# Attention kernel with gated experts on one core: the value products one head further behind, two casts moved to ScalarE, the first half's sums moved on VectorE

## The chip, the cores and the metric

The kernel runs on one core of one Trainium2 chip. The metric is the device time of one launch in microseconds (us); lower is better. The engines are TensorE (PE in the rows, PEld its weight loads), VectorE (DVE), ScalarE (ACT), GpSimd (POOL) and SyncE (SP), which issues the DMAs.

## What is computed

For 16 batch items of 256 tokens by 256 features, four residual stages, each added to x:

```
x = x + x @ weight[subject].T + bias[subject]
x = x + zX*lap_x(x) + zY*lap_y(x) + zR*x*(1 - x)        # reflected edges
x = x + attention(x, side)    # 16 heads of 16; keys: the masked previous 256 and the token itself
x = x + sum_e w_e * relu(x @ wi_e) @ wo_e               # 2 shared experts and 1 chosen, hidden 1024
        # w = softmax(relu(gate_in @ g1) @ g2), gate_in from token 0 of the three experts
attention: softmax over [q k_prev^T * SCALE (masked), q.k_self * SCALE], times [v_prev, v_self], @ Wo + bo
```

## The kernel before

**Stages and turns.** One pass of the loop is a turn. A turn works on three batch items at once: the inputs, the first two stages and q, k, v of item i; the attention of item i-1 (scores `S0` to `S15`, exponentials `E0` to `E15`); and the experts of item i-2 (`H0` to `H11` the hidden products, `P0` to `P11` the projections). The function `lag` says which item a name belongs to. Turns 0 and 1 are written out, turns 2 to 15 run in a hardware loop, turns 16 and 17 empty the pipeline.

**What sets the order.** Each engine has its own list of names (`PE_BODY`, `ACT_BODY`, `DVE_BODY`, `POOL_BODY`, `SP_BODY`) and works it off strictly from left to right; semaphores join the lists. Nothing is reordered.

**A head.** TensorE makes the transposed scores of head h (`E`, line 665, two matmuls) into one of two PSUM banks. ScalarE takes the exponential twice: to `prob` in f32 (line 869) and to `prob_hi` in f16 (line 873). VectorE (line 1054) or GpSimd (line 1269) subtracts the two into `prob_lo`. For the heads in `HI_DVE` ScalarE takes it only once, and VectorE casts `prob` to `prob_hi` (line 1053) ahead of the subtraction. The tuple `LO_DVE` holds the heads whose `prob_lo` VectorE makes; the other nine are GpSimd's. There are three buffers of each (`NPROB`), taken in turn by h % 3. The function `attend` multiplies head h by the values: eight matmuls of 49 columns (lines 607 and 608, "pv" in the rows), which wait for `prob_lo` of h. It is called right behind `E` of head h + `BEHIND`, and `pvend` calls it for the heads that are left over.

**Banks.** The two front banks go round in the order of TensorE's list (`RING`): `E14` uses the bank in which `kp` stood, and waits until VectorE has read that (line 1014, `beside<-front`). `kp` uses the bank of `E11`; `E11` that of `lap`.

**The first half's sums.** `half` on VectorE (lines 1062, 1065, 1067) reads the value products of heads 0 to 7 from PSUM. It waits for `attend` of head 7. `attend` of head 8 writes over the same PSUM and waits for `half` (the semaphore `pv_freed`). `lap` on VectorE (line 1003) adds the Laplacian from PSUM to `react`; `x2_parts` (line 976) then splits the result of the second stage, on which TensorE's `kp` waits.

**GpSimd's list** in this part of the turn is `E8 E9 E10 qa E12 norm qb E14`: four subtractions of `prob_lo`, two of q (lines 1230 and 1233), and the first half's normalisation (lines 1259 and 1263).

The lists around the change, before:

```
PE   ... m1 E7 x1 P7 q E8 H9 E9 lap P8 E10 H10 E11 E12 kp E13 P9 E14 E15 H11 P10 pvend P11 vs ...
ACT  ... x1_parts react q E8 P7 H9 E9 x2_parts E10 qa H10 E11 E12 kp E13 qb kq E14 E15 H11 P11 ...
```

Of the kernel before, what the change touches and what calls it, by code (L numbers as in the profile page):

```python
# [67 lines left out]
ACT_FIRST = "x_parts w_parts s_parts x1_parts react q qa x2_parts qb kp kq vs ks vp x2b".split()  # L68
DVE_BODY = """
H0 S0 S1 H1 S2 S3 S4 S5 H2 S6 S7 S8 S9 H3 S10 S11 H4 H5 S12 S13 E1 S14 H6 S15 E3 H7 E5 gate0 x_parts H8 E7  # L70
x1 x1_parts react half lap H9 x2_parts gate1 E11 H10 kp E13 k3 E15 H11
att gate2 aT relu wo logits x3_parts mix scale vp self
""".split()
POOL_BODY = """
# [20 lines left out]
def family(name):  # L95

    if name in FAMILIES:
        return name, 0
    return (name[0], int(name[1:])) if name[0] in FAMILIES and name[1:].isdigit() else (None, 0)
# [23 lines left out]


NPROB = 3
BEHIND = 2
HI_DVE = (11, 13, 15)
LO_DVE = (1, 3, 5, 7) + HI_DVE
N_LO_DVE = [sum(g in LO_DVE for g in range(h + 1)) for h in range(H)]
N_LO_POOL = [h + 1 - N_LO_DVE[h] for h in range(H)]  # L130

# [2 lines left out]

LINKS = {"early": 3, "attention": 4 + 5 + len(HI_DVE), "rest": 8}


def wait(eng, sem, per_turn, turn, n):

    value = turn * per_turn + n  # L140
    if isinstance(value, int) and value <= 0:
        return
    eng.wait_ge(sem, value)


def build(nc, x, side, seq_len, subject, label, z, w0, b0, wqkvo, vecs, wi, wo, swi, swo,
          g1, g2, consts, iota, out):
    with ExitStack() as ctx:
# [204 lines left out]
        def wait_freed(eng, i, name):  # L353
            kind, n = family(name)
            wait(eng, freed[kind], FAMILIES[kind], i, n + 1)

        def wait_prob_split(eng, i, h):

            if h in LO_DVE:
                wait(eng, prob_split_dve, N_LO_DVE[-1], i, N_LO_DVE[h])  # L360
# [186 lines left out]
        def _(pe):  # L547
# [48 lines left out]
            def attend(i, h):  # L596

                wait_prob_split(pe, i, h)
                if h == 0:
                    wait(pe, v_split, 1, i, 1)  # L600
                if h == HALF:
                    wait(pe, pv_freed, 1, i, 1)
                for t in range(C):
                    acc = pv[:, t, (h % HALF) * VW:(h % HALF + 1) * VW]
                    for k in range(C):
                        at = k * S + t * P
                        nc.tensor.matmul(acc, prob_hi[:, h % NPROB, at:at + P], v_cols[:, k, h, :], start=(k == 0), stop=False)  # L607
                        last = nc.tensor.matmul(acc, prob_lo[:, h % NPROB, at:at + P], v_cols[:, k, h, :],
                                                start=False, stop=(k == C - 1))
                last.then_inc(pv_done, 1)  # L610

            def front(name, i):
                if name == "pvend":
                    for h in range(H - BEHIND, H):
                        attend(i, h)
# [51 lines left out]
                last.then_inc(filled[family(name)[0]], 1)  # L667
                if name[0] == "E" and int(name[1:]) >= BEHIND:
                    attend(i, int(name[1:]) - BEHIND)

# [117 lines left out]
        def _(act):  # L788
            def front(name, i):
# [73 lines left out]
                elif name[0] == "E":  # L863
# [5 lines left out]
                    last = nc.scalar.activation(prob[:, h % NPROB, :], psum[:, :], ACT.Exp, scale=SCALE)  # L869
                    if h not in HI_DVE:  # L870
                        if h >= NPROB:
# [89 lines left out]
        def _(dve):  # L961
# [9 lines left out]
            def front(name, i):  # L971
# [76 lines left out]
                elif name[0] == "E":  # L1048
                    h = int(name[1:])
                    wait_freed(dve, i, name)  # L1050
                    if h in HI_DVE:
                        wait(dve, pv_done, H, i, h - NPROB + 1)
# [290 lines left out]
```

## Time and profile before

| what | value |
| --- | --- |
| time, median of 3 runs | 1078.11 us (1074.57 to 1078.93) |
| the profiled execution, its own time | 1079.35 us |
| its span, first to last instruction | 1077.5 us |
| PE busy | 993.3 us, 92% |
| DVE busy | 828.2 us, 77% |
| ACT busy | 670.6 us, 62% |
| POOL busy | 623.9 us, 58% |
| one turn in the dense part (540.0 to 602.8 us) | 62.8 us, of which PE is busy 60.24, DVE 51.01, ACT 41.18, POOL 37.74 |
| granted TensorE clock in it | 1.00 of full |

Matmuls overlap in the engine, so the start of one to the start of the next is what it costs, not its duration. A row of the timeline gives a start, a duration, and in square brackets how long the engine had sat idle before it and what ended that.

### The profile page before, as it was taken

Reading aid. Unit: us, or ns where it says so; the run is one execution under the profiler, and the core shown is the slowest. Engines: PE = TensorE matmul, PEld = TensorE weight load, DVE = VectorE, ACT = ScalarE, POOL = GpSimd, SP = SyncE. Lnnn points to the kernel's source line nnn. Section 1 sums busy time; section 2 is a strip of 40 time slices with the busy share of each in tenths; the row PEclk is TensorE's granted clock in tenths of the full one; section 3 lists DMA queues with packets and bytes.
Section 4 is the critical chain, followed back from the end, with each engine's and each line's share of the span. In section 5 each row is a group of like instructions: output and inputs, shape, how many; then the busy total and the mean of one; then the engine's idle time right before and its main releaser. Section 6 shows DMA issues by size and latency. Waiting matters only on the chain.

```text
span 1077.5 us, 27626 instructions
## 1 busy us (share of the span) xinstructions
PE 993.3 (92%) x9488; PEld 926.5 (86%) x9488; DVE 828.2 (77%) x1584; ACT 670.6 (62%) x1403; POOL 623.9 (58%) x548
## 2 busy tenths in 40 slices
PE   5669999999999999999999999999999999999896
PEld 5358989898998989899898989989898998989886
DVE  6566787878878787887878788787878878787633
ACT  4464756667485666748566674856667485666641
POOL 5683646567374656737465673746567374655440
PEclk8568999999999999999999999999999999999988
DMA  6626142531614253162425316242531614252110
GB/s 159 164 71 118 51 60 79 91 85 46 111 59 59 79 90 86 45 110 61 59 79 90 86 44 111 61 59 79 88 88 44 110 62 59 79 89 59 41 49 10
DMA packets 91387, 82.68 MB, mean 77 GB/s; under 512 B 11972, under 2 KB 90852, under 8 KB 91364
## 3 DMA queue, kind: packets, MB, share of 16 engines
q1 hardware_dynamic: 91364, 82.38, 35.7%
q8 instruction: 14, 0.23, 0.1%
q14 instruction: 9, 0.07, 0.0%
HBM read 52.59 MB, written 4.20 MB: 53 GB/s over the span
## 4 chain that ended last, share of the span: by engine, by line
PE 33%; issue 25%; POOL 22%; DVE 14%; ACT 3%; SPq 1%; DMA 1%; POOLq 0%; DVEq 0%; ACTq 0%
POOL exp_lo L1212 12%; PE front L550 3%; PE hid L550 3%; PE front L552 3%; PE front L551 3%; POOL prob_lo L1269 3%; PE hid L552 3%; PE hid L551 3%; PE out L550 3%; PE out L552 3%; PE out L551 3%; DVE gate_terms L1133 2%; DVE prob_lo L1054 2%; DVE prob_hi L1053 2%; PE pv L607 2%
## 5 line engine op out<-in xcount | busy, mean ns | idle before, releaser
L1269 POOL TENSOR_TENSOR prob_lo<-prob,prob_hi 128x512 f16<-128x512 f32 x144 | 174.4, 1211 | 108.6 <-ACT prob_hi L873 108.6
L550 PE MATMUL hid<-x_hi,exp_hi 128*128 128x256 f32 x768 | 230.1, 300 | 1.5 <-DVE x_lo L1114 1.5
L550 PE MATMUL out<-hid_hi,exp_hi 128*128 128x256 f32 x768 | 228.2, 297 | 0.0
L551 PE MATMUL hid<-x_lo,exp_hi 128*128 128x256 f32 x768 | 217.1, 283 | 0.0
L552 PE MATMUL hid<-x_hi,exp_lo 128*128 128x256 f32 x768 | 216.9, 282 | 0.0
L551 PE MATMUL out<-hid_lo,exp_hi 128*128 128x256 f32 x768 | 214.7, 280 | 0.0
L552 PE MATMUL out<-hid_hi,exp_lo 128*128 128x256 f32 x768 | 214.6, 279 | 0.0
L1212 POOL TENSOR_TENSOR exp_lo<-raw,exp_hi 128x512 fp32r<-128x512 f32 x128 | 169.3, 1337 | 70.3 <-ACT exp_hi L890 70.2
L1034 DVE TENSOR_REDUCE s_max<-front 128x2 f32<-128x512 f32 x256 | 167.7, 687 | 46.2 <-PE front L652 44.2
L912 ACT ACTIVATE hid_hi<-hid 128x512 fp32r<-128x512 f32 x192 | 114.8, 598 | 111.6 <-PE hid L552 110.3
L1118 DVE SCALAR_TENSOR_TENSOR hid_lo<-hid,hid_hi 128x512 fp32r<-128x512 f32 x192 | 131.6, 685 | 64.5 <-ACT hid_hi L912 64.2
L869 ACT ACTIVATE prob<-front 128x512 f32<-128x512 f32 x256 | 151.4, 598 | 39.6 <-PE front L665 36.8
L550 PEld LDWEIGHTS hid<-x_hi,exp_hi 128*128 128x128 f32 x768 | 145.6, 190 | 4.0 <-DVE x_lo L1114 1.6
L550 PEld LDWEIGHTS out<-hid_hi,exp_hi 128*128 128x128 f32 x768 | 144.4, 188 | 3.2 <-DVE hid_lo L1118 0.2
L551 PEld LDWEIGHTS hid<-x_lo,exp_hi 128*128 128x128 f32 x768 | 146.1, 190 | 0.0
L552 PEld LDWEIGHTS hid<-x_hi,exp_lo 128*128 128x128 f32 x768 | 145.6, 190 | 0.0
L551 PEld LDWEIGHTS out<-hid_lo,exp_hi 128*128 128x128 f32 x768 | 144.8, 189 | 0.0
L552 PEld LDWEIGHTS out<-hid_hi,exp_lo 128*128 128x128 f32 x768 | 144.3, 188 | 0.0
L1054 DVE TENSOR_TENSOR prob_lo<-prob,prob_hi 128x512 f16<-128x512 f32 x112 | 113.6, 1014 | 31.2 <-ACT prob_hi L873 29.5
L607 PEld LDWEIGHTS pv<-v_cols,prob_hi 128*128 128x128 f16 x1024 | 70.6, 97 | 65.3 <-DVE prob_lo L1054 36.5
L607 PE MATMUL pv<-v_cols,prob_hi 128*128 128x49 bf16 x1024 | 87.2, 187 | 42.2 <-DVE prob_lo L1054 27.7
L873 ACT ACTIVATE prob_hi<-front 128x512 f16<-128x512 f32 x208 | 125.0, 601 | 0.0
(166 smaller groups left out, 2329.0 us busy)
## 6 DMA issues: line engine op xcount, KB each, us to landing
raw<-in_wi SPq DMA_DIRECT2D x64, 256.0 KB, 3.7
raw<-in_wo SPq DMA_DIRECT2D x64, 256.0 KB, 2.8
q_rows<-w_raw SPq DMA_DIRECT2D x80, 128.0 KB, 4.0
k_rows<-x1T SPq DMA_DIRECT2D x48, 128.0 KB, 5.0
k_rows<-x_raw SPq DMA_DIRECT2D x48, 128.0 KB, 6.1
x_raw<-in_x SPq DMA_DIRECT2D x16, 256.0 KB, 2.9
w_raw<-in_w SPq DMA_DIRECT2D x16, 256.0 KB, 2.8
s_raw<-in_side SPq DMA_DIRECT2D x16, 256.0 KB, 3.7
```

The lines of the kernel that those rows point to most:

```text
L550: nc.tensor.matmul(acc, w_hi, a_hi, start=first, stop=False)
L551: nc.tensor.matmul(acc, w_hi, a_lo, start=False, stop=False)
L552: return nc.tensor.matmul(acc, w_lo, a_hi, start=False, stop=last)
L607: nc.tensor.matmul(acc, prob_hi[:, h % NPROB, at:at + P], v_cols[:, k, h, :], start=(k == 0), stop=False)
L869: last = nc.scalar.activation(prob[:, h % NPROB, :], psum[:, :], ACT.Exp, scale=SCALE)
L873: last = nc.scalar.activation(prob_hi[:, h % NPROB, :], psum[:, :], ACT.Exp, scale=SCALE)
L912: nc.scalar.activation(hid_hi[:, s % 2, :], hid_bank[s % 2][:, :], ACT.Relu).then_inc(hid_hi_done, 1)
L1034: nc.vector.tensor_reduce(s_max[:, :, h:h + 1], psum, AX_X, ALU.max).then_inc(freed["S"], 1)
L1054: nc.vector.tensor_tensor(prob_lo[:, h % NPROB, :], prob[:, h % NPROB, :], prob_hi[:, h % NPROB, :], ALU.subtract).then_inc(prob_split_dve, 1)
L1118: nc.vector.scalar_tensor_tensor(hid_lo[:, s % 2, :], hid_bank[s % 2][:, :], 0.0, hid_hi[:, s % 2, :].bitcast(F32), ALU.max, ALU.subtract) ...
L1212: nc.gpsimd.tensor_tensor(lo, source, hi.bitcast(F32), ALU.subtract).then_inc(w_split, 1)
L1269: nc.gpsimd.tensor_tensor(prob_lo[:, h % NPROB, :], prob[:, h % NPROB, :], prob_hi[:, h % NPROB, :], ALU.subtract).then_inc(prob_split_poo ...
```

## The change

`BEHIND` goes from 2 to 3, so that `attend` of head h stands behind `E` of head h+3, and `pvend` holds three heads, not two. Heads 13 and 15 leave `HI_DVE`: ScalarE takes their second exponential into `prob_hi`, and VectorE no longer casts them; `LO_DVE` is unchanged in content. `half` moves on VectorE's list from in front of `lap` to behind `H9`.

```
-x1 x1_parts react half lap H9 x2_parts gate1 E11 H10 kp E13 k3 E15 H11
+x1 x1_parts react lap H9 half x2_parts gate1 E11 H10 kp E13 k3 E15 H11
...
 NPROB = 3
-BEHIND = 2
-HI_DVE = (11, 13, 15)
-LO_DVE = (1, 3, 5, 7) + HI_DVE
+BEHIND = 3
+HI_DVE = (11,)
+LO_DVE = (1, 3, 5, 7, 11, 13, 15)
```

VectorE in the loop, around `lap` (L1003), `H9` (L1118), the first half's sums (L1062 to L1067) and `x2_parts` (L976):

```order
+L1003 SCALAR_TENSOR_TENSOR react<-front,z_sb,react 128x512
+L143 REGISTER_ALU
+L1118 SCALAR_TENSOR_TENSOR hid_lo<-hid,hid_hi 128x512
 L1062 TENSOR_REDUCE att<-pv 128x128 x2
 L1065 TENSOR_TENSOR den<-pv,p_self 128x2x8
 L1067 RECIPROCAL den<-den 128x2x8
-L1003 SCALAR_TENSOR_TENSOR react<-front,z_sb,react 128x512
-L143 REGISTER_ALU
-L1118 SCALAR_TENSOR_TENSOR hid_lo<-hid,hid_hi 128x512
 L976 TENSOR_TENSOR x_lo<-react,x_hi 128x512
```

Two operations that stood behind the sums now stand ahead of them; `x2_parts` keeps its place right behind.

VectorE in the loop, from the reading of `kp` (L1014, `beside`) on, heads 13 and 15:

```order
 L1014 SCALAR_TENSOR_TENSOR beside<-front,ebias,x1T 128x256 x2
-L1053 CAST prob_hi<-prob 128x512
-L143 REGISTER_ALU
 L1054 TENSOR_TENSOR prob_lo<-prob,prob_hi 128x512
 L143 REGISTER_ALU
...
 L1020 TENSOR_TENSOR x_raw<-beside,x_raw 128x256
-L1053 CAST prob_hi<-prob 128x512
-L143 REGISTER_ALU
 L1054 TENSOR_TENSOR prob_lo<-prob,prob_hi 128x512
```

The two casts behind `kp` are gone; the cast of head 11, ahead of it, stays.

ScalarE in the loop, head 13 behind the two parts of `kp`, ahead of `qb` (L822) and `kq` (L838):

```order
 L869 ACTIVATE prob<-front 128x512
+L873 ACTIVATE prob_hi<-front 128x512
 L822 ACTIVATE w_raw<-s_raw 128x512
 L838 ACTIVATE x_raw<-beside 128x256 x2
...
 L869 ACTIVATE prob<-front 128x512
+L873 ACTIVATE prob_hi<-front 128x512
 L143 REGISTER_ALU
 L912 ACTIVATE hid_hi<-hid 128x512
```

One more exponential stands ahead of `qb` (head 13) and one ahead of `H11` (head 15).

## Rows read from the trace of the kernel before

**Rows 1.** The page: busy time by engine, and the costliest-groups row of line 607.

```profile
PE 993.3 (92%) x9488; PEld 926.5 (86%) x9488; DVE 828.2 (77%) x1584; ACT 670.6 (62%) x1403; POOL 623.9 (58%) x548
...
L607 PE MATMUL pv<-v_cols,prob_hi 128*128 128x49 bf16 x1024 | 87.2, 187 | 42.2 <-DVE prob_lo L1054 27.7
```

**Rows 2.** Timeline of PE: start, duration, operation, [idle before it and releaser].

```profile
138.91 0.20 PE L607 MATMUL pv<-v_cols,prob_hi 128*128 128x49 bf16 x1 [1.03 <-DVE prob_lo L1054]
...
560.62 0.38 PE L665 MATMUL front<-q_rows,k_rows 100*128 100x256 bf16 x2
561.14 0.20 PE L607 MATMUL pv<-v_cols,prob_hi 128*128 128x49 bf16 x1
...
573.03 0.19 PE L607 MATMUL pv<-v_cols,prob_hi 128*128 128x49 bf16 x1
...
575.88 0.20 PE L607 MATMUL pv<-v_cols,prob_hi 128*128 128x49 bf16 x1 [0.30 <-POOL prob_lo L1269]
...
579.03 0.20 PE L607 MATMUL pv<-v_cols,prob_hi 128*128 128x49 bf16 x1 [1.01 <-DVE prob_lo L1054]
...
580.75 0.39 PE L665 MATMUL front<-q_rows,k_rows 100*128 100x256 bf16 x2
580.98 0.19 PE L607 MATMUL pv<-v_cols,prob_hi 128*128 128x49 bf16 x1
...
582.32 0.20 PE L607 MATMUL pv<-v_cols,prob_hi 128*128 128x49 bf16 x1 [0.75 <-DVE prob_lo L1054]
...
582.54 0.35 PE L550 MATMUL hid<-x_hi,exp_hi 128*128 128x256 f32 x1
...
585.88 0.36 PE L550 MATMUL out<-hid_hi,exp_hi 128*128 128x256 f32 x1
...
956.26 0.20 PE L607 MATMUL pv<-v_cols,prob_hi 128*128 128x49 bf16 x1 [1.03 <-DVE prob_lo L1054]
```

**Rows 3.** Timeline of DVE in the same turn, from the first half's sums on.

```profile
570.87 0.56 DVE L1062 TENSOR_REDUCE att<-pv 128x128 f32<-128x384 f32 x1 [0.26 <-PE pv L608]
...
572.17 0.66 DVE L1003 SCALAR_TENSOR_TENSOR react<-front,z_sb,react 128x512 f32<-128x512 f32 x1
...
573.53 0.88 DVE L976 TENSOR_TENSOR x_lo<-react,x_hi 128x512 fp32r<-128x512 f32 x1
...
574.84 1.26 DVE L1133 SCALAR_TENSOR_TENSOR gate_terms<-gate,e_out,gate_terms 128x256 f32<-128x256 f32 x1
...
576.13 1.28 DVE L1053 CAST prob_hi<-prob 128x512 f16<-128x512 f32 x1
577.44 1.53 DVE L1054 TENSOR_TENSOR prob_lo<-prob,prob_hi 128x512 f16<-128x512 f32 x1
...
579.50 0.86 DVE L1014 SCALAR_TENSOR_TENSOR beside<-front,ebias,x1T 128x256 f32<-128x256 f32 x2
```

**Rows 4.** Timeline of POOL in turn 1 (first row) and in the same turn as rows 2.

```profile
76.22 0.73 POOL L1259 TENSOR_TENSOR att<-att,v_self 128x256 f32<-128x256 f32 x1
...
574.54 1.27 POOL L1269 TENSOR_TENSOR prob_lo<-prob,prob_hi 128x512 f16<-128x512 f32 x1 [0.69 <-ACT prob_hi L873]
575.78 1.34 POOL L1230 TENSOR_TENSOR s_raw<-q_full,w_raw 128x512 f32<-128x512 f32 x1
577.10 1.32 POOL L1269 TENSOR_TENSOR prob_lo<-prob,prob_hi 128x512 f16<-128x512 f32 x1
578.39 1.17 POOL L1259 TENSOR_TENSOR att<-att,v_self 128x256 f32<-128x256 f32 x1
579.64 0.40 POOL L1263 TENSOR_TENSOR att<-att,den 128x128 f32<-128x128 f32 x1
```

**Rows 5.** Timeline of ACT in the same turn, the second exponential of head 12.

```profile
576.40 0.62 ACT L873 ACTIVATE prob_hi<-front 128x512 f16<-128x512 f32 x1
```

**Rows 6.** Timeline of PE in turn 1, the first with attention.

```profile
50.76 0.22 PE L607 MATMUL pv<-v_cols,prob_hi 128*128 128x49 bf16 x1 [2.38 <-POOL prob_lo L1269]
...
78.54 0.28 PE L665 MATMUL front<-q_rows,k_rows 100*128 100x256 bf16 x1 [1.27 <-DVE beside L1014]
```

## The prediction

> **What bounds the kernel now.** The page first: TensorE is busy 92% of the span and no other engine more than 77% [rows 1]. Idle time on TensorE is therefore what a reordering can win. The costliest single wait of it is ahead of the value products, 42.2 us in all, 27.7 of them for a `prob_lo` of VectorE [rows 1]. The timeline of TensorE over one turn then shows where. Four waits come back in every turn: 0.29 us ahead of the products of head 4 (its `E6` starts at 560.62 and costs 0.23, as from 580.75 to 580.98, yet the products start only at 561.14), 0.30 for head 10, 1.01 for head 11, 0.75 for head 13 [rows 2]. That is 2.35 us of a turn. The wait of head 11 stands in 14 turns, the first at 138.91 and the last at 956.26: 13 periods of 62.87 us [rows 2]. Everything else in those turns has TensorE packed, so a turn costs what its path from wait to wait costs. The four waits together are 14 x 2.35 = 33 us, the most that the change could take away in the dense part.
>
> **What goes.** With `attend` one head further behind, each of the four waits meets a `prob_lo` that was made one head earlier, and all four go. For that to be a gain, the work behind them must be ready earlier too. Up to `E10` it is: the lists there are TensorE-driven, and I shift everything by the 0.29 of head 4. From `E10` on, the path goes over to VectorE, for which I follow one turn in the trace's own times.
>
> **The path from the half's sums to `E14`.** The products behind `E10`, at 573.03 before [rows 2], are now those of head 7, at 572.74. Their eight matmuls need 0.36 us to the end, and the semaphore 0.1: `half` can start at 573.20. Before, it started at 570.87 [rows 3]. `lap` and `H9` now run ahead of it, but VectorE has only those two (0.66 and 0.68 us) to fill the time, so it stands idle for about 1.5 us where it had idled 0.26. `half` costs 572.17 - 570.87 = 1.30 us [rows 3], and so `x2_parts` may begin at 574.50, against 573.53 before. (`pv_freed` comes inside those 1.30 us, and the products of head 8 want it at 574.70. No stall there, with 0.2 us to spare. ScalarE's second exponential waits for the products of head h-3, which now stand behind its own `E`: they are done 0.36 us behind `E`, and the first exponential takes longer than that.)
>
> What comes then is the costly part, because GpSimd works without a gap from 574.54 to 580.0 [rows 4], and VectorE operations on SBUF operands do not run beside it. The cast at 576.13 took 1.28 us: it ended at 577.41, 0.29 us after GpSimd's operation ended (575.78 + 1.34 = 577.12). The subtraction at 577.44 ended at 578.97, 0.55 us after 577.10 + 1.32 = 578.42. The gate term at 574.84 ended 0.29 after 574.54 + 1.27 [rows 3, 4]. So each such operation costs the rest of GpSimd's operation, then 0.29 or 0.55 us. Operations that read PSUM (`half`, `H10`, the reading of `kp`) keep their length.
>
> GpSimd's own times: its subtraction for head 10 moves from 574.54 to 574.17, since `x2_parts` on ScalarE no longer holds up that head's exponentials. Unhindered it would last 1.17 us, to 575.34. Then:
>
> - `x2_parts`, ready at 574.50, waits for 575.34 and ends at 575.89. TensorE's `kp` starts at 575.99, against 576.10 (575.88 and 0.22 of products) before [rows 2]: so far 0.11 us won out of the first 0.59 of waits.
> - The first gate term waits for GpSimd's `qa`, 575.31 + 1.34 [rows 4] = 576.65, perhaps 0.25 more as it had to let a 512-wide operation by. It ends at 577.0 to 577.2. Before, this one ran freely.
> - The second gate term meets the subtraction of head 12. That depends on ScalarE's exponential (576.40, now 0.28 earlier: ended 576.74 [rows 5]) and on `qa`, and runs to about 578.05. The term ends at 578.35.
> - The cast of head 11 meets the addition of `norm`. That took 1.17 us where it let a subtraction by, and 0.73 in turn 1 [rows 4]; I take 0.8, to 578.9. The cast ends at 579.2.
> - The subtraction of head 11 meets one of the two 0.40 us multiplications of `norm` [rows 4], to about 579.35, and ends at 579.9.
> - From there to the end of reading `kp` it is, as before, 579.50 + 0.86 - 578.97 = 1.39 us [rows 3]: 581.29. The casts that are taken away (heads 13 and 15) stand behind this point, so they give nothing here.
>
> `E14` on TensorE needs that bank, and starts at 581.33, against 580.75. TensorE, which has won 2.35 us of waits, gets to it at about 579.4 and stands there for 1.9 us. This is the new wait.
>
> **From `E14` to `P11`.** Before: 585.88 - 580.75 = 5.13 us, 0.75 of it the wait for head 13 [rows 2]. Now `E14` and `E15` at 0.23 each, two products at 0.21, then `H11` and `P10` (585.88 - 582.54 = 3.34, with two products in it) and one more product, 0.21: 4.43 us. `P11` starts at 581.33 + 4.43 = 585.76, against 585.88. On the way VectorE must have `hid_lo` of `H11` ready: its two casts less pay for ScalarE's additional exponential of head 15 (0.6 us), and I find it ready at 585.5, so it is covered by 0.3 us. ScalarE has 62.8 - 41.2 us free in a turn; the two exponentials more hide there. Net: 0.12 us won in a turn, 14 x 0.12 = 1.7 us. The break-even is `E14` at 581.45, and nearly every microsecond of the forecast hangs on whether the chain above ends before or after it.
>
> **The ends.** Turn 1 is not dense: TensorE waits 2.38 us for the first subtraction with `E3` stuck behind it, and 1.27 us at `E14` [rows 6]. There `E3` comes up to 1.4 us earlier (the exponential of head 3 needs only the buffer of head 0), and `lap` ahead of `half` gives `E11` 0.7 us. Bounds 0 and 4, I take 2.5 us. The last attention turn has few waits left: 0.3 us.
>
> **The sum.** 1.7 + 2.5 + 0.3 = 4.5 us. On the profiled execution's own 1079.35 us (span 1077.5 and 1.85 around it) that gives 1074.9; it lies 1.2 above the median of the runs, 1078.11, from which it is **1073.6 us**.
>
> **The rule on the shared port.** The rows above show VectorE waiting for GpSimd's whole operation. The Trainium skill, page "SBUF — State Buffer", section "SBUF: two separate sides", states it for both sides: the pair of ports is an exclusive lock, held for the full instruction, and the loser blocks entirely. The trace agrees for VectorE; for GpSimd it does not quite, since the operation next to the cast took 1.32 us and not the 1.16 + 0.3 of a full block [rows 4].
>
> **Rivals.**
>
> 1. *VectorE's chain ends later (slower).* Each VectorE operation that squeezes in holds GpSimd up by its whole 0.3 to 0.55 us, not by 0.1 to 0.2, and the five operations of the stretch add about 1 us: `E14` at 582.3. From `E14` at 582.0 on, the loss in 14 turns outweighs 0.5% and the gain of the ends. At 582.3 it is 14 x 0.85 - 2.8 = 9 us lost: 1087. For it: GpSimd has no gap in the stretch, and one more of its operations (`qb`, 1.3 us) waits behind. Against: the 1.32 above. By that rule of the Trainium skill ("SBUF — State Buffer") in its full form, this would be the case. Chance 0.2.
> 2. *One VectorE operation escapes.* A gate term or the cast that starts before GpSimd's next operation does runs in 0.4 us; the cast spent 0.99 us of its 1.28 waiting [rows 3, 4]. Then the path is 0.9 shorter: 14 x 0.9 more, 1061 to 1064. For it: the second gate term and the subtraction of head 12 start within 0.2 us of each other. Chance 0.23. Without any such waits `E14` would be bound by TensorE, 14 x 2.1 + 3: 1046; I leave that out.
> 3. *The waits only change place.* The four go, `E14` takes up all of them, turn 1 is bound by GpSimd as before: 1078. Chance 0.15.
>
> The forecast itself has 0.42, with a range of 1069 to 1078.
>
> **Numbers.** A measurement of this kernel can tell about 0.5% from no change, which is 5.4 us: 1072.7 and 1083.5. Faster by more: all of rival 2 and a little less than half of the forecast's own, 0.42. Slower by more: rival 1, 0.2. Within: the rest, 0.38. The range reaches from rival 2 to short of the worst of rival 1: 1063 to 1086.
>
> **What would show it.** In the changed trace: the four waits of the value products gone from TensorE's list, and in their place one wait per turn of `front` (line 665) for VectorE's `beside` (line 1014), 1.9 us by this sum. VectorE idle about 0.8 us ahead of the sums of line 1062. The gate terms and the cast between them at 1.2 us each, not 0.4. The period of a turn at 62.7 us: above 63.0 is rival 1, under 62.2 is rival 2. The forecast falls if `kp` or the products of head 8 wait instead (the 0.2 us to spare on `pv_freed` is the thinnest cover), or if `P11` comes to wait for `hid_lo`.

## The result, and the profile after

The changed kernel takes 1086.73 us in the median of 5 runs (1083.17 to 1087.27), against 1075.93 for the kernel before in the same comparison (5 runs). The ratio is 1.0086, with a 95% interval of 1.0061 to 1.0110: slower by 0.9%. The forecast was 1073.6 and its range ended at 1086. The profiled execution has a span of 1085.4 us, against 1077.5.

From the page of the changed kernel, the busy time and the group that now has the large wait (the same columns as in [rows 1]):

```profile
PE 997.6 (92%) x9488; PEld 943.5 (87%) x9488; DVE 800.5 (74%) x1552; ACT 683.4 (63%) x1435; POOL 628.6 (58%) x548
...
L665 PE MATMUL front<-q_rows,k_rows 100*128 100x256 bf16 x512 | 102.3, 282 | 39.7 <-DVE beside L1014 29.6
```

VectorE is busy 28 us less, ScalarE 13 more: the casts moved. The 42.2 us ahead of the value products [rows 1] are no longer the largest wait. The list of waits of TensorE says what took their place (in total, times, longest):

```profile
PE front L665 <- DVE beside L1014: 29.6, 15, 2.1
PE front L550 <- DVE x_lo L976: 9.7, 15, 2.1
...
PE front L658 <- DVE s_max L1034: 5.7, 15, 2.0
```

That is one wait per turn at `E14` (line 665) and one at `kp` (line 550). The wait at `kp` is new too: 0.55 us a turn. The forecast's numbers hold one of about 0.5 (0.59 us won ahead of it, and `kp` only 0.11 earlier), though its list of signs names a wait at `kp` as one that would make it fall. In the timeline of TensorE, one dense turn of the changed kernel reads as follows; it is the turn to be laid beside [rows 2], with `kp`, `E14`, `H11`, `P10` and `P11`:

```profile
579.49 0.35 PE L550 MATMUL front<-x_hi,lin_hi 128*128 128x256 f32 x1 [0.55 <-DVE x_lo L976]
...
585.09 0.39 PE L665 MATMUL front<-q_rows,k_rows 100*128 100x256 bf16 x2 [2.01 <-DVE beside L1014]
...
585.94 0.51 PE L550 MATMUL hid<-x_hi,exp_hi 128*128 128x256 f32 x1
...
588.60 0.41 PE L550 MATMUL out<-hid_hi,exp_hi 128*128 128x256 f32 x1
...
591.01 0.37 PE L550 MATMUL out<-hid_hi,exp_hi 128*128 128x256 f32 x1
```

So far this is the forecast: the four waits are gone, and one of 2.01 us (1.9 was written) stands at `E14`. Then something the forecast does not have: `H11` to `P10`, twelve matmuls of 256 columns, takes 588.60 - 585.94 = 2.66 us. Before, it took 584.03 - 582.54 [rows 2] = 1.49, with `P10` starting in this row of the kernel before:

```profile
584.03 0.28 PE L550 MATMUL out<-hid_hi,exp_hi 128*128 128x256 f32 x1
```

The windows show why. They cover the pause, the 3.4 us that begin 0.9 us behind it, and 3.4 us later on; the columns are busy us of PE, PEld, DVE, ACT and POOL with the instructions, then the granted clock, the DMA share and GB/s:

```profile
584.00:585.00 1.00, 0.00 (x0) 0.00 (x0) 1.00 (x4) 0.00 (x0) 1.00 (x1) 1.00 0.00 0
586.00:589.40 3.40, 3.40 (x20) 3.40 (x17) 1.09 (x2) 2.29 (x5) 1.17 (x1) 0.50 0.54 112
590.00:593.40 3.40, 3.40 (x49) 3.36 (x48) 2.18 (x8) 0.66 (x2) 0.00 (x0) 1.00 1.14 127
```

TensorE is idle while VectorE and GpSimd work. Then its granted clock is 0.50 (1.2 GHz) for 3.4 us, in which it is called fully busy, yet a matmul of 256 columns starts every 0.22 us (2.66 / 12) instead of every 0.12 (1.49 / 12). (The 49 matmuls of the last window can't be set against the 20: many of them are value products of 49 columns.) `E14` to `P11` takes 591.01 - 585.09 = 5.92 us, against the 4.43 of the forecast, which all belonged to the full clock. Not every turn has this. `E14` of five successive turns, the last but one being the row at 585.09 above:

```profile
393.90 0.28 PE L665 MATMUL front<-q_rows,k_rows 100*128 100x256 bf16 x1 [2.01 <-DVE beside L1014]
...
458.13 0.28 PE L665 MATMUL front<-q_rows,k_rows 100*128 100x256 bf16 x1 [2.01 <-DVE beside L1014]
...
522.36 0.28 PE L665 MATMUL front<-q_rows,k_rows 100*128 100x256 bf16 x1 [2.00 <-DVE beside L1014]
...
649.30 0.28 PE L665 MATMUL front<-q_rows,k_rows 100*128 100x256 bf16 x1 [2.00 <-DVE beside L1014]
```

The distances are 64.23, 64.23, 62.73 and 64.21 us. A turn without the slow stretch takes 62.7 us, and one with it 1.5 us more; 10 of the 14 turns from 2 to 15 have one. In the kernel before none of these turns has one, and a turn takes 62.87. The slow stretch does not begin at a fixed distance from the pause: in the ten turns it begins 0.4 to 1.6 us behind the pause's end.

The account of the 7.9 us between the two spans, with a turn counted from the first matmul of `x1`: up to the x1 stage of turn 2, 3.4 us are won (120.33 us instead of 123.75). In the next 13 turns, 9 slow stretches cost 9 x 1.52 = 13.7 us and the shorter path wins 13 x 0.16 = 2.1. The rest (turn 15, with the tenth slow stretch, and the emptying of the pipeline) is 0.3 us shorter. -3.4 + 13.7 - 2.1 - 0.3 = 7.9.

VectorE's chain in the same turn, for [rows 3], and GpSimd's subtraction of head 10, `qa` and subtraction of head 12, for [rows 4]:

```profile
576.60 1.02 DVE L1062 TENSOR_REDUCE att<-pv 128x128 f32<-128x384 f32 x2 [0.60 <-PE pv L608]
...
577.90 1.43 DVE L976 TENSOR_TENSOR x_lo<-react,x_hi 128x512 fp32r<-128x512 f32 x1
579.26 2.69 DVE L1133 SCALAR_TENSOR_TENSOR gate_terms<-gate,e_out,gate_terms 128x256 f32<-128x256 f32 x2
581.99 0.85 DVE L1053 CAST prob_hi<-prob 128x512 f16<-128x512 f32 x1
582.87 0.77 DVE L1054 TENSOR_TENSOR prob_lo<-prob,prob_hi 128x512 f16<-128x512 f32 x1
...
584.17 0.86 DVE L1014 SCALAR_TENSOR_TENSOR beside<-front,ebias,x1T 128x256 f32<-128x256 f32 x2
```

```profile
577.63 1.16 POOL L1269 TENSOR_TENSOR prob_lo<-prob,prob_hi 128x512 f16<-128x512 f32 x1 [0.62 <-ACT prob_hi L873]
578.75 1.62 POOL L1230 TENSOR_TENSOR s_raw<-q_full,w_raw 128x512 f32<-128x512 f32 x1
580.33 1.34 POOL L1269 TENSOR_TENSOR prob_lo<-prob,prob_hi 128x512 f16<-128x512 f32 x1
```

`x_lo` takes 1.43 us instead of 0.88: GpSimd's subtraction, already running, ends at 577.63 + 1.16 = 578.79, and `x_lo` 0.54 later. The two gate terms take 2.69 us together, behind `qa` and the subtraction of head 12 in the same way. This is as the forecast had it. From the start of the sums (576.60) to the end of reading `kp` (585.03) it is 8.43 us; the walk of the prediction had 581.29 - 573.20 = 8.09.

### The profile page after: what moved, and what is told of

It reads as the page before. It is cut to its first block, busy times and chain, and to the rows that moved or that the text cites. A ratio compares the mean times of both kernels' runs of the same rounds, so it can differ in the third digit from the quotient of the medians.

```text
span 1085.4 us, 27581 instructions
## 1 busy us (share of the span) xinstructions
PE 997.6 (92%) x9488; PEld 943.5 (87%) x9488; DVE 800.5 (74%) x1552; ACT 683.4 (63%) x1435; POOL 628.6 (58%) x548
## 4 chain that ended last, share of the span: by engine, by line
PE 73%; DVE 18%; issue 3%; POOL 2%; ACT 1%; DMA 1%; SPq 1%; DVEq 0%; ACTq 0%
PE hid L550 8%; PE hid L551 8%; PE hid L552 7%; PE out L550 7%; PE out L552 7%; PE out L551 7%; PE front L665 5%; PE front L652 4%; PE front L550 4%; DVE gate_terms L1133 3%; PE front L552 3%; PE front L551 3%; DVE s_max L1034 3%; PE pv L607 2%; DVE x_lo L976 2%
## 5 line engine op out<-in xcount | busy, mean ns | idle before, releaser
L550 PE MATMUL hid<-x_hi,exp_hi 128*128 128x256 f32 x768 | 234.2, 305 | 1.8 <-DVE x_lo L1114 1.8
L551 PE MATMUL hid<-x_lo,exp_hi 128*128 128x256 f32 x768 | 221.3, 288 | 0.0
L552 PE MATMUL hid<-x_hi,exp_lo 128*128 128x256 f32 x768 | 221.1, 288 | 0.0
L1118 DVE SCALAR_TENSOR_TENSOR hid_lo<-hid,hid_hi 128x512 fp32r<-128x512 f32 x192 | 131.7, 686 | 72.1 <-ACT hid_hi L912 71.1
L550 PEld LDWEIGHTS hid<-x_hi,exp_hi 128*128 128x128 f32 x768 | 149.1, 194 | 4.3 <-DVE x_lo L1114 1.9
L551 PEld LDWEIGHTS hid<-x_lo,exp_hi 128*128 128x128 f32 x768 | 150.3, 196 | 0.0
L552 PEld LDWEIGHTS hid<-x_hi,exp_lo 128*128 128x128 f32 x768 | 149.9, 195 | 0.0
L873 ACT ACTIVATE prob_hi<-front 128x512 f16<-128x512 f32 x240 | 144.9, 604 | 0.0
L665 PE MATMUL front<-q_rows,k_rows 100*128 100x256 bf16 x512 | 102.3, 282 | 39.7 <-DVE beside L1014 29.6
L1054 DVE TENSOR_TENSOR prob_lo<-prob,prob_hi 128x512 f16<-128x512 f32 x112 | 92.1, 823 | 47.0 <-ACT prob_hi L873 45.1
L1236 POOL TENSOR_TENSOR ksT<-ksT,q_full 128x512 f32<-128x512 f32 x16 | 20.4, 1278 | 129.4 <-ACT ksT L808 129.4
```

The costliest lines, as they stand in the source:

```text
L550: nc.tensor.matmul(acc, w_hi, a_hi, start=first, stop=False)
L551: nc.tensor.matmul(acc, w_hi, a_lo, start=False, stop=False)
L552: return nc.tensor.matmul(acc, w_lo, a_hi, start=False, stop=last)
L665: last = nc.tensor.matmul(psum[:, k * S:(k + 1) * S], k_rows[0:ROWS_EXP, h, k * P:(k + 1) * P], q_rows[0:ROWS_EXP, h, :], start=True, stop ...
L873: last = nc.scalar.activation(prob_hi[:, h % NPROB, :], psum[:, :], ACT.Exp, scale=SCALE)
L1054: nc.vector.tensor_tensor(prob_lo[:, h % NPROB, :], prob[:, h % NPROB, :], prob_hi[:, h % NPROB, :], ALU.subtract).then_inc(prob_split_dve, 1)
```

## The experiments

Theories. **Clock**: the loss is the slow stretch of TensorE behind the new pause. **Path**: the loss is VectorE's longer chain itself (rival 1 of the prediction), and the clock is only a companion. Ratios are against the kernel before in the same comparison. "Slow stretches" counts turns 2 to 15 with a stretch of granted clock 0.50, in the one profiled execution of each kernel. Each median is of 3 to 10 executions, but of 2 for e10_fill_behind, e13_fill_far and e14_pause, and the two of e14_pause lie 6.7 us apart.

| kernel | median us | ratio, 95% interval | slow stretches of 14 | dense turn, us |
| --- | --- | --- | --- | --- |
| before | 1075.9 | 1 | 0 | 62.87 |
| changed | 1086.7 | 1.0086 (1.0061 to 1.0110) | 10 | 62.7 or 64.2 |
| e1_fill | 1071.3 | 0.9941 (0.9920 to 0.9961) | 0 | 62.7 |
| e9_fill_4 | 1071.8 | 0.9949 (0.9933 to 0.9965) | 0 | 62.7 |
| e10_fill_behind | 1103.7 | 1.0246 (1.0225 to 1.0267) | 3 | 64.7 or 66.2 |
| e13_fill_far | 1101.6 | 1.0243 (1.0213 to 1.0273) | 11 | 63.7 or 65.2 |
| e14_pause | 1101.8 | 1.0245 (1.0171 to 1.0319) | 5 | 63.8 or 65.3 |
| e5_no_casts | 1087.8 | 1.0095 (1.0079 to 1.0112) | 10 | 62.9 or 64.2 |
| e6_half_back | 1098.5 | 1.0195 (1.0178 to 1.0212) | 10 | 63.8 to 65.7 |
| e7_half_alone | 1083.2 | 1.0050 (1.0033 to 1.0067) | 0 | 63.1 |
| e3_casts | 1063.5 | 0.9879 (0.9863 to 0.9896) | 0 | 61.9 |
| e8_all_casts | 1061.2 | 0.9858 (0.9841 to 0.9874) | 0 | 61.7 |
| e2_h11_ahead | 1069.0 | 0.9922 (0.9905 to 0.9938) | 0 | 62.46 |
| e4_gate1_later | 1068.5 | 0.9917 (0.9900 to 0.9933) | 0 | 62.42 |
| e11_h11_everywhere | 1081.9 | 1.0046 (1.0032 to 1.0060) | 7 | 62.55 or 64.0 |
| e12_casts_gate1 | 1074.1 | 0.9976 (0.9966 to 0.9985) | 0 | 62.6 |

### The pause filled

On TensorE, in turns 2 to 15, ahead of `E14`:

```
+FILL = 16
...
+                if name == "E14" and not isinstance(seq, int):
+                    for _ in range(FILL):
+                        nc.tensor.matmul(hid_bank[1][:, 0:S], lap_mats[:, 0:P], lap_mats[:, :], start=True, stop=True)
```

> The changed kernel with 16 extra matmuls (128x256, f32r, constants, result overwritten by the next hidden product) between P9 and E14 in turns 2 to 15, where TensorE pauses for 2.0 us. They do no work for the result and end before the pause did. Clock theory (the loss is that the granted clock falls to 1.2 GHz behind this pause in two of three turns, which costs 1.5 us each time): the clock stays at 1.00 through turns 2 to 15, every turn takes 62.7 us instead of 64.2, and the time falls by about 10 x 1.5 = 15 us to some 1071. Path theory (the loss is the later end of VectorE's chain): E14 starts where it did, nothing changes, 1086. If the filler ends too late, turns are a few tenths longer in both.

It came out at 1071.3 us, on the expectation of the clock theory. `E14` starts 18.07 us behind the first matmul of `x1`, where it also started in the changed kernel (585.09 - 567.01 = 18.08), but no pause is left ahead of it (line numbers are up to 4 higher in kernels with a filler):

```profile
513.77 0.39 PE L666 MATMUL front<-q_rows,k_rows 100*128 100x256 bf16 x2
```

The granted clock over the dense turns, in windows, e1_fill:

```profile
130.00:960.00 830.00, 816.15 (x8071) 780.45 (x8069) 652.85 (x1273) 553.21 (x1177) 504.04 (x437) 1.00 0.37 75
```

and the changed kernel:

```profile
130.00:960.00 830.00, 792.00 (x7707) 756.83 (x7707) 641.57 (x1251) 545.77 (x1160) 495.35 (x431) 0.98 0.36 75
```

TensorE does 224 more matmuls for nothing, and the kernel is 15 us faster, because the clock is 1.00 and not 0.98. VectorE's chain is as long as before. The path theory falls with this run: with the clock kept up, the change as a whole is a gain of 0.6% (0.4% to 0.8%), and the 4.5 us of the prediction, 0.42%, lie at the near end of that.

### A smaller filler, and two controls

Four extra matmuls instead of 16:

```
-FILL = 16
+FILL = 4
```

> As the filled kernel, with 4 extra matmuls in the pause instead of 16, so that about 1.55 us of the 2.0 us pause are left, in one piece. If the clock falls on the length of the pause in steps, the count of 1.2 GHz stretches in turns 2 to 15 lies between the 10 of the changed kernel and the 0 of the filled one, and the time between 1071 and 1086 at 1.5 us for each stretch; E14 starts where it did in both.

No slow stretch at all, with 1.55 us of the pause left:

```profile
514.38 0.28 PE L666 MATMUL front<-q_rows,k_rows 100*128 100x256 bf16 x1 [1.55 <-DVE beside L1018]
```

So 0.45 us of work in the pause bought 15 us. The expectation of something in between was wrong: 14 pauses of 1.55 us lowered the clock in no turn.

The same 16 behind `E14`, outside the pause:

```
-                if name == "E14" and not isinstance(seq, int):
+                if name == "E15" and not isinstance(seq, int):
```

> The control to the filled kernel: the same 16 extra matmuls per turn, but between the products behind E14 and E15, so the pause of 2.0 us ahead of E14 stays whole. Clock theory (the pause, not the amount of work in a turn): the 1.2 GHz stretches come back in most turns; a turn takes 62.7 + 1.9 = 64.6 us without one and 1.5 to 3 more with one: 1110 to 1118. If more work in a turn alone kept the clock up: 64.6 in every turn, 1098.

```profile
529.00 0.28 PE L666 MATMUL front<-q_rows,k_rows 100*128 100x256 bf16 x1 [2.04 <-DVE beside L1018]
```

The pause is whole, and the slow stretches are back, but only 3, and the time of 1103.7 lies between the two expectations. That left open whether more work in a turn also protects. A second control has 8 extra matmuls ahead of `H4`, 28 us from the pause:

```
+FILL = 8
...
+                if s == 4 and not isinstance(j, int):
+                    for _ in range(FILL):
+                        nc.tensor.matmul(psum[:, 0:S], lap_mats[:, 0:P], lap_mats[:, :], start=True, stop=True)
```

> A second control: the changed kernel with 8 extra matmuls (0.95 us) ahead of H4 in turns 2 to 15, some 28 us away from the pause ahead of E14, which stays 2.0 us. Clock theory (what stands in the pause matters): 1.2 GHz stretches in most turns again, 7 to 11 of 14, turns of 63.7 us without and 65.2 with one, time about 1100. If more work anywhere in a turn protected the clock: none, 63.7 in every turn, 1085.

```profile
528.56 0.37 PE L666 MATMUL front<-q_rows,k_rows 100*128 100x256 bf16 x1 [2.00 <-DVE beside L1018]
```

11 slow stretches and 1101.6 us, as the clock theory expects. More work in a turn does not protect by itself; work in the pause does. Why the same pause of 2.0 us lowered the clock 10 or 11 times in three kernels, but 3 times in the control with the filler right behind it, is not settled. One thing that no run here varied by itself is the length of a turn (62.7 to 64.7 us in these kernels), and with it where the pause falls in time.

### The converse

In the kernel with the two casts alone (below), TensorE waits ahead of `E14` for VectorE's `k3`, in turns 2 to 15:

```
+                if name == "E14" and not isinstance(seq, int):
+                    wait(pe, k_split, 1, seq + 1, 1)
```

> The converse, in the fastest kernel but one (the kernel before with the two casts on ScalarE): TensorE waits ahead of E14 for VectorE's k3, which ends about 1.9 us after TensorE gets there; nothing else is changed, BEHIND is 2. Clock theory: one pause of about 2 us makes 1.2 GHz stretches in many of turns 2 to 15 where there were none; a turn is 61.9 + 1.9 = 63.8 us without one and 1.5 more with one, time 1097 to 1104. If the clock fell in the changed kernel for another reason (its order of products, say), no stretches here: 1090.

```profile
523.70 0.20 PE L607 MATMUL pv<-v_cols,prob_hi 128*128 128x49 bf16 x1 [1.04 <-DVE prob_lo L1056]
...
527.31 0.28 PE L665 MATMUL front<-q_rows,k_rows 100*128 100x256 bf16 x1 [1.74 <-DVE x_raw L1022]
```

The added pause is 1.74 us long, in a kernel with `BEHIND` 2 and the sums where they were, and 5 slow stretches come where there were none. It does not stand alone: the wait of 1.04 us for head 11 ends at 523.70, and the pause begins 1.9 us later, so the run shows what the two do together. A turn is 63.8 us without a slow stretch and 65.3 with one, the same 1.5 us. Most of what this kernel loses against the casts alone (38 us in the medians) is the pause itself, 14 x 1.9 = 27 us by the turns; the five stretches are about 8.

### The parts of the change

The casts alone (`BEHIND` 2, `half` ahead of `lap`):

```
-HI_DVE = (11, 13, 15)
-LO_DVE = (1, 3, 5, 7) + HI_DVE
+HI_DVE = (11,)
+LO_DVE = (1, 3, 5, 7, 11, 13, 15)
```

> The kernel before with one part of the change alone: the high parts of heads 13 and 15 on ScalarE; BEHIND stays 2 and the sums stay ahead of the Laplacian. By the trace of before: VectorE's subtraction of head 13 starts at once behind the reading of kp and ahead of GpSimd's qb, so it ends about 1 us earlier and the wait of 0.75 us ahead of the products of head 13 goes; nothing behind it is later. Clock theory: the waits left are 0.3, 0.3 and 1.0 us, the clock stays at 1.00, and the turn falls to about 62.1: 14 x 0.75, time about 1066. Path theory: the same, since VectorE's path is shorter. If instead this part is the harmful one, slower than before, since ScalarE's qb and kq are 0.5 us later: 1080 or more.

1063.5 us: 1.2% faster than before, and better than expected. In VectorE's timeline of the kernel with the casts alone, the subtraction of head 13 takes 0.68 us right behind the reading of `kp`:

```profile
510.71 0.86 DVE L1014 SCALAR_TENSOR_TENSOR beside<-front,ebias,x1T 128x256 f32<-128x256 f32 x2
511.49 0.68 DVE L1054 TENSOR_TENSOR prob_lo<-prob,prob_hi 128x512 f16<-128x512 f32 x1
```

It begins just ahead of GpSimd's `qb` and does not wait for it; behind the cast it had waited. The wait of 0.75 us at head 13 [rows 2] is gone, and the turn is 0.95 us shorter.

The other two parts without the casts:

```
-HI_DVE = (11,)
-LO_DVE = (1, 3, 5, 7, 11, 13, 15)
+HI_DVE = (11, 13, 15)
+LO_DVE = (1, 3, 5, 7) + HI_DVE
```

> The changed kernel with the casts of heads 13 and 15 back on VectorE: the one further head behind and the moved sums alone. VectorE's chain up to the reading of kp is untouched by those casts, so the pause ahead of E14 stays 2.0 us and the granted clock falls behind it in most turns. Clock theory: as slow as the changed kernel, 1084 to 1089; the 0.95 us per turn that the casts alone gave is hidden under the wait for the bank. Path theory with the casts as an independent gain: 13 us slower than the changed kernel, about 1100.

```profile
PE front L665 <- DVE beside L1014: 29.5, 15, 2.1
```

1087.8 us, as slow as the changed kernel (1086.7), with the same wait. The casts, worth 13 us alone, are worth about 1 us inside the change, which the intervals do not tell from nothing: the pause at `E14` hides what they save. The slow stretch costs 1.3 us here, 64.25 us against 62.95.

One head further behind, with the sums back ahead of the Laplacian:

```
-x1 x1_parts react lap H9 half x2_parts gate1 E11 ...
+x1 x1_parts react half lap H9 x2_parts gate1 E11 ...
```

> The changed kernel with the sums back ahead of the Laplacian, one head further behind kept. VectorE then waits for the products of head 7 (now behind E10) before it can do lap, about 2.6 us idle, and E11, x2_parts on ScalarE, the exponentials of head 10 and kp come later by 0.7 to 1.5 us. Dense turns of 64 us without clock falls; with pauses ahead of E11, kp and E14 that add up to 4 us the clock also falls in most turns: 1100 to 1110. If the moved sums were what cost the time, it would be faster than the changed kernel: 1075 or less.

```profile
PE front L665 <- ACT prob_hi L873: 20.7, 22, 1.3
PE front L550 <- ACT prob L869: 12.2, 14, 0.9
PE front L665 <- DVE react L1003: 10.7, 15, 2.4
```

1098.5 us, 1.5 under the expected range. `E11` waits for `lap` (0.6 us a turn), `E12` and `kp` for ScalarE (1.04 and 0.90), and the clock falls in 10 turns, behind the second of these waits or behind the third. In 4 of the 10 the slow stretch lasts 6.8 us and not 3.4. So the moved sums are needed once the products are three heads behind.

The moved sums alone, in the kernel before:

```
-x1 x1_parts react half lap H9 x2_parts gate1 E11 ...
+x1 x1_parts react lap H9 half x2_parts gate1 E11 ...
```

> The kernel before with the moved sums alone. The products of head 8, behind E10, now wait about 0.9 us for the sums, which start 1.9 us later than before; x2_parts and the gate terms meet GpSimd's operations one place later, so the reading of kp is later by up to 1 us and shows in the wait of head 11. Dense turns of 63.6 to 64 us, no single pause over 1.3 us, so the clock stays at 1.00: 1088 to 1094.

```profile
PE pv L607 <- DVE den L1065: 13.5, 15, 2.5
PE pv L607 <- DVE prob_lo L1054: 11.1, 31, 1.1
```

The wait for the sums is there (0.81 us a turn), but the turn is only 0.25 us longer and not 0.7 to 1.1, since part of the later waits for `prob_lo` falls under it (11.1 us left of them). 1083.2, and no slow stretch. The expectation overstated what follows.

### Towards a faster kernel

All three casts on ScalarE, `BEHIND` 2:

```
-HI_DVE = (11, 13, 15)
-LO_DVE = (1, 3, 5, 7) + HI_DVE
+HI_DVE = ()
+LO_DVE = (1, 3, 5, 7, 11, 13, 15)
```

> The kernel before with the casts of all three heads, 11, 13 and 15, on ScalarE (the last run's faster part, taken one head further). The cast of head 11 costs VectorE 1.3 us there, 1.0 of it waiting for GpSimd; without it the subtraction of head 11 ends about 1.3 us earlier and the wait of 1.0 us ahead of its products goes. ScalarE's and GpSimd's head 12 come 0.5 us later, which is covered. Dense turns of about 60.9 us, time about 1049. If ScalarE's additional exponential delays qb, kq or head 12 by more than their cover, 1063 as with two casts.

1061.2 us, the fastest of all, 1.4% under the kernel before. But only 0.2 us a turn came of the 1.0 expected. The wait at head 11 is gone, and `kp` comes to wait, since its bank is free only behind the second exponential of head 11. That is 0.3 us a turn, and `P11` waits another 0.2 for `hid_lo`; the rest of the shortfall is not accounted for.

```profile
PE front L550 <- ACT prob_hi L873: 4.3, 14, 0.3
```

`H11` ahead of `E14`, on TensorE only:

```
-... kp E13 P9 E14 E15 H11 P10 pvend P11
+... kp E13 P9 H11 E14 E15 P10 pvend P11
```

> The changed kernel with TensorE's H11 moved ahead of E14 (P9 H11 E14 E15 P10), so that real work of 1.5 us stands in the pause; the lists of the other engines are unchanged. Both theories: the pause ahead of E14 falls from 2.0 to about 0.6 us, and P11 comes to wait about 1.2 us for hid_lo of H11, which VectorE and ScalarE still have behind E15; P11 starts 4.2 us behind E14 instead of 4.4. Clock theory: two short pauses do not lower the clock, turns of 62.4 us, time about 1067. Path theory: only the 0.25 us per turn, 1083.

```profile
512.23 0.28 PE L665 MATMUL front<-q_rows,k_rows 100*128 100x256 bf16 x1 [0.58 <-DVE beside L1014]
```

1069.0 us, close to the 1067 expected: real work fills the pause as well as the filler does. `P11` waits 0.29 us for `hid_lo` and not the 1.2 expected.

The gate terms behind `k3`, in the changed kernel:

```
-... half x2_parts gate1 E11 H10 kp E13 k3 E15 H11
+... half x2_parts E11 H10 kp E13 k3 gate1 E15 H11
```

> The changed kernel with VectorE's gate1 (two gate terms, 2.7 us in the chain while GpSimd works) moved from behind x2_parts to behind k3, so that the reading of kp is earlier. Both theories: E14 comes 1.5 to 2 us earlier, its pause shrinks to under 0.5 us, and the dense turns fall to about 61 us if nothing behind E14 is late (gate1 now stands ahead of E15, so the products of head 15 or P11 may wait a few tenths). Clock theory: the clock stays at 1.00, 14 x 1.7 and 10 x 1.5 us less than the changed kernel: about 1048. Path theory: only the 14 x 1.7, 1062.

```profile
PE front L665 <- DVE beside L1014: 9.5, 15, 1.4
PE pv L607 <- DVE prob_lo L1054: 7.9, 15, 0.6
...
PE out L550 <- DVE hid_lo L1118: 4.1, 14, 0.3
```

`E14` comes 1.4 us earlier, its wait shrinks to 0.57, and the clock stays up. Yet the turn falls by 0.3 us only. The end of the turn takes the gain back: the products of head 15 wait 0.55 us and `P11` 0.29. The forecast of 1048 had called this "a few tenths", and it was the new bound. What ends a turn is ScalarE's and VectorE's chain for heads 14 and 15.

Both moves, with `H11` early on all three engines:

```
-PE  ... P9 E14 E15 H11 P10 pvend   ACT ... qb kq E14 E15 H11   DVE ... x2_parts gate1 E11 H10 kp E13 k3 E15 H11
+PE  ... P9 H11 E14 E15 P10 pvend   ACT ... qb kq H11 E14 E15   DVE ... x2_parts E11 H10 kp E13 k3 gate1 H11 E15
```

> The changed kernel with gate1 behind k3 and H11 ahead of E14 on TensorE and ScalarE and ahead of E15 on VectorE. Nothing of TensorE is left to wait for the bank of kp; the products of head 15 wait about 0.8 us for the chain of ScalarE's two last exponentials and VectorE's subtraction, and P11 no longer for hid_lo. The clock stays at 1.00. Dense turns of 61.3 us, about 1052. If the last head's chain is a microsecond later than that (H11 now stands ahead of it on ScalarE), 62.4 us and 1068, as the two kernels that moved one thing.

```profile
518.35 0.20 PE L607 MATMUL pv<-v_cols,prob_hi 128*128 128x49 bf16 x1 [0.34 <-POOL prob_lo L1269]
...
520.05 0.20 PE L607 MATMUL pv<-v_cols,prob_hi 128*128 128x49 bf16 x1 [1.33 <-DVE prob_lo L1054]
```

1081.9 us. The chain of head 15 ends 0.5 us later than hoped, so two pauses, 0.34 and 1.33 us, lie close together, and behind them the clock falls in 7 of 14 turns. A kernel whose turn is 62.55 us at full clock is slower than the one before with 62.87, for the same reason as the change.

The casts with the gate terms behind `k3`, `BEHIND` 2:

```
-... half lap H9 x2_parts gate1 E11 H10 kp E13 k3 E15 H11
+... half lap H9 x2_parts E11 H10 kp E13 k3 gate1 E15 H11
```

> The kernel before with the two casts on ScalarE and gate1 behind k3, BEHIND 2 and the sums ahead of the Laplacian. The gate terms (1.8 us here) no longer stand ahead of the subtraction of head 11, so its wait of 1.0 us goes; they now stand ahead of head 15, where ScalarE's exponentials are the later ones by 0.8 us. Dense turns of 61.0 us, about 1051; 1063 if the end of the turn takes the gain back.

```profile
511.93 1.10 DVE L1053 CAST prob_hi<-prob 128x512 f16<-128x512 f32 x1 [1.60 <-ACT prob L869]
513.06 1.59 DVE L1054 TENSOR_TENSOR prob_lo<-prob,prob_hi 128x512 f16<-128x512 f32 x1
```

1074.1 us, 10.6 slower than the casts alone and above both expected times (1051 and 1063). Without the gate terms ahead of it, the cast of head 11 is not earlier: VectorE stands idle for 1.60 us until ScalarE's exponential, and both operations then meet GpSimd as before. The gate terms had been free there, and now stand in the way of head 15.

## Why the prediction was wrong

**What held.** TensorE as the bound, and the four waits of 2.35 us that go: all four went. The walk along VectorE: the sums start 573.20 - 563.57 = 9.63 us into the turn by the forecast, and 9.59 in the trace (563.57 is the first matmul of `x1` in the trace of before, 563.86, less the 0.29 of head 4); the pause at `E14` was to be 1.9 us and is 2.01; a turn at full clock was to take 62.75 us and takes 62.7. Turn 1 was to give 2.5 us and, counted up to the x1 stage of turn 2, gave 3.4. The sum of the prediction, 4.5 us won, is within the interval of what e1_fill measures: a ratio of 0.9941 (0.9920 to 0.9961), about 6 us.

That 62.75 and 62.7 agree so well is partly luck. `E14` came 18.07 us behind the first matmul of `x1` and not 17.76 (581.33 - 563.57), so it was 0.3 us late. `P11` to the next `x1` took 40.24 us against 40.85 before, 0.6 less, where the forecast had taken off only the 0.29 of head 4. Part of it is a slip in the sum: with three heads in `pvend`, one head's products (0.21 us) no longer stand behind `E2`. The sum added them between `E14` and `P11`, and did not take them off where they had stood.

**The step that failed** is "From `E14` to `P11`": the 4.43 us were added up from rows at granted clock 1.00, without asking whether the clock would still be 1.00 behind a pause that the same paragraph put at 1.9 us. It was 0.50 for 3.4 us in 10 of 14 turns, and the term measured 5.92 us in the one shown; at full clock it measured 4.40 (522.36 to 526.76), as forecast. That is about 15 us in all, more than three times the whole forecast gain. The rows to ask with were in the trace of before: its four waits a turn, the longest 1.0 us, never lowered the clock in turns 2 to 15, but the change was about to replace them by one of twice the length.

The Trainium skill, page "TensorE: Matmul & The Clock Gate", section "Part 1: The HAM clock gate", says that an idle TensorE is put to half its clock and that activity releases it. The runs agree in direction. The drops here came behind one pause of 2.0 us (e13_fill_far, say), and also behind several shorter ones that stood close together, none over 1.04 us, in e6_half_back.

**The rivals.** Rival 1 gave 1087, and 1086.7 was measured, but its mechanism (GpSimd held up, `E14` at 582.3 instead of 581.33, a dense turn of 63.7 in every turn) is not what happened: `E14` came 0.3 us later than forecast, and e1_fill, with the same VectorE chain, takes 1071.3. The loss has another cause of the same size. Rival 2, an operation that escapes GpSimd, did not occur in the changed kernel; in e3_casts it did, for the subtraction of head 13. Rival 3 is close to what the dense turns do at full clock (62.7 against 62.87).

**The account of the casts.** The prediction said that they give nothing ahead of `E14`. That was right inside the change (e5_no_casts), but they were by far the best part alone (e3_casts). The chances of 0.42, 0.38 and 0.20 were of the full-clock path, and none of them held a case for the clock.

## What to carry to other kernels

Idle time on a dense TensorE does not simply add up. In the kernel before, four waits of 0.3 to 1.0 us spread over a turn never lowered the clock, while one of 2.0 us in the changed kernel cost another 1.5 us through the clock in 10 turns of 14. When a reordering gathers small waits into one large one, price the stretch behind it at both clocks, and look for work to put into it; here 0.45 us of anything was enough. And measure the parts of a change apart: one of these three was worth more than the whole was meant to bring, and the new pause hid it.

## What the runs showed of the hardware

- A pause of 2.0 us in a TensorE that is otherwise nearly always busy was followed by 3.4 us at granted clock 0.50, in 10 of 14 turns (changed kernel, e5_no_casts), 11 of 14 (e13_fill_far) and 3 of 14 (e10_fill_behind). The slow stretch began at the earliest 0.1 us before the pause ended (e10_fill_behind), at the latest 1.6 us behind its end (changed kernel). Each cost 1.5 us of the turn (1.3 in e5_no_casts).
- The length of the longest pause alone does not decide it. One of 1.55 us lowered the clock in no turn (e9_fill_4), one of 1.74 with 1.04 shortly ahead of it in 5 (e14_pause), one of 1.33 with 0.34 shortly ahead of it in 7 (e11_h11_everywhere), and three of 0.6, 1.0 and 0.9 within 4 us in 10 (e6_half_back).
- VectorE's subtractions, casts and gate terms, when they start during a GpSimd operation, end 0.3 to 0.55 us behind it: `x_lo` 0.54 behind 578.79, the cast of head 11 0.29 behind 577.12 [rows 3, 4]. The GpSimd operation that follows is lengthened too, by less than that: `qa` takes 1.62 us behind `x_lo` and 1.17 in e12_casts_gate1, where nothing of VectorE's ends beside it. A subtraction takes 1.32 us next to the cast [rows 4], and 1.16 at 577.63 in the changed kernel.
